# Two attention layers on one core: convolutions in idle score banks, a projection spread over the second layer, and the eighth chunk's values made in the next image

## What is computed

```python
# layer 0: 32-channel q and k, 256-channel v, softmax over axis 1
q = einsum('oc,bcn->bon', Wq, xf) + bq;  k = ... Wk;  v = ... Wv
attn = softmax(einsum('bci,bcj->bij', q, k), axis=1)
x = gamma * einsum('bcn,bnm->bcm', v, attn) + xf
# layer 1: phi and g are pooled 2x2, so that there are 1024 keys
theta = conv1x1(x);  phi = maxpool2(conv1x1(x));  g = maxpool2(conv1x1(x))
attention = softmax(theta^T phi, axis=-1)
y = gamma * conv1x1(g . attention) + x
```

## Time and profile before

| | |
|---|---|
| median of 3 runs (lowest, highest) | 2952.17 us (2945.66, 2953.29) |
| profiled execution, whole | 2952.56 us |
| its span, first to last instruction | 2950.8 us |
| mean granted TensorE clock | 0.967 of full |
| PE busy | 2757.0 us (93%) |
| DVE, POOL, ACT busy | 2008.1, 1949.9, 1750.7 us |
| longest waits of PE, in total | for prob_l 37.0 us, for vl 25.7 us, for psums 20.0 us |

### The profile page before, as it was taken

One profiled execution on the slowest core, in us unless ns is written; L12 is line 12 of the kernel. 1 busy time (PEld: TensorE's weight loads), 2 busy tenths in 40 slices (PEclk: granted clock), 3 DMA queues, 4 the chain that ended last, 5 costly groups with the idle time before them and its releaser, 6 DMA issues.

```text
span 2950.8 us, 39091 instructions
## 1 busy us (share of the span) xinstructions
PE 2757.0 (93%) x12260; PEld 2180.1 (74%) x12260; DVE 2008.1 (68%) x3303; ACT 1750.7 (59%) x3171; POOL 1949.9 (66%) x1480
## 2 busy tenths in 40 slices
PE   5899999989999999998999999999799999999978
PEld 4677777766677777776667777777666777777756
DVE  4577767756767677675776776777576767777665
ACT  3455565555665655555676565565566556555657
POOL 2366666765676667764677677666567766666658
PEclk7799999998999999999899999999999999999989
DMA  2000000011210000001120000000111000000011
GB/s 88 22 15 15 15 15 15 22 36 36 72 50 15 15 15 22 22 15 36 51 68 34 15 22 22 15 15 15 44 58 58 23 21 15 15 15 15 15 35 65
DMA packets 44280, 87.10 MB, mean 30 GB/s; under 512 B 2736, under 2 KB 2864, under 8 KB 44080
## 3 DMA queue, kind: packets, MB, share of 16 engines
q1 hardware_dynamic: 35360, 68.17, 6.8%
q10 hardware_dynamic: 8720, 16.46, 1.9%
HBM read 51.06 MB, written 33.55 MB: 29 GB/s over the span
## 4 chain that ended last, share of the span: by engine, by line
PE 77%; issue 9%; DVE 5%; ACT 5%; POOL 4%; DMA 1%; POOLq 0%; ACTq 0%; DVEq 0%
PE o_ps L797 30%; PE o_ps L775 16%; PE s_ps L765 8%; PE aux L828 8%; POOL prob_l L427 3%; PE aux L808 3%; PE aux L841 2%; ACT prob_h L490 2%; DVE mx L650 2%; PE aux L837 2%; PE aux L845 1%; PE aux L812 1%; PE aux L862 1%; PE o_ps L828 1%; PE o_ps L862 1%
## 5 line engine op out<-in xcount | busy, mean ns | idle before, releaser
L427 POOL TENSOR_TENSOR prob_l<-prob,prob_h 128x512 fp32r<-128x512 f32 x1280 | 1639.7, 1289 | 751.6 <-ACT prob_h L490 744.2
L487 ACT ACTIVATE prob<-s_ps 128x512 f32<-128x512 f32 x1280 | 768.5, 600 | 974.2 <-PE s_ps L765 973.5
L650 DVE TENSOR_REDUCE mx<-aux 128x1 f32<-128x512 f32 x1115 | 769.5, 690 | 459.3 <-PE aux L828 458.0
L797 PE MATMUL o_ps<-prob_h,vh 128*128 128x512 f32 x2304 | 935.8, 406 | 17.5 <-issue 12.6
L797 PE MATMUL o_ps<-prob_h,vl 128*128 128x512 f32 x2304 | 904.6, 393 | 0.0
L612 DVE TENSOR_TENSOR acc<-prob,acc 128x512 f32<-128x512 f32 x1216 | 836.1, 688 | 45.4 <-ACT prob L487 34.2
L775 PE MATMUL o_ps<-prob_l,vh 128*128 128x512 f32 x2304 | 756.0, 400 | 37.4 <-POOL prob_l L427 37.0
L490 ACT ACTIVATE prob_h<-s_ps 128x512 fp32r<-128x512 f32 x1280 | 762.1, 595 | 0.0
L775 PEld LDWEIGHTS o_ps<-prob_l,vh 128*128 128x128 f32 x2304 | 437.4, 191 | 144.7 <-POOL prob_l L427 57.0
L797 PEld LDWEIGHTS o_ps<-prob_h,vh 128*128 128x128 f32 x2304 | 437.0, 190 | 124.3 <-issue 24.8
L765 PE MATMUL s_ps<-queries,keys 128*128 128x512 f32 x1280 | 509.2, 399 | 0.8 <-DVE queries L669 0.8
(11 more groups left out here) (91 smaller groups left out, 1997.9 us busy)
## 6 DMA issues: line engine op xcount, KB each, us to landing
xa<-x SPq DMA_DIRECT2D x32, 512.0 KB, 3.7
...
```

Source lines behind the costliest of these rows:

```text
L427: nc.gpsimd.tensor_tensor(out=prob_l[:, i, :], in0=prob[:, i, :], in1=prob_h[:, i, :].bitcast(f32), op=ALU.subtract).then_inc(pl_ready, 1)
L487: nc.scalar.activation(prob[:, i, :], s_ps[s][:, :], ACT.Exp).then_inc(p_ready, 1)
L650: ins = nc.vector.tensor_reduce(out=dst, in_=bank[:, :], axis=AX.X, op=ALU.max)
L797: last = mm(o_ps[ct][:, :], value(parts, l, t, ct), prob_h[:, h % RING, :], start=t == 0 and parts is vh, stop=False)
```

## The change

The work is the same: every engine has as many instructions of each kind, except that four loads of image 0 (its chunks 0 to 3, which were loaded into `xa` as well as into `xp`) fall away.

1. **Banks.** Jobs in the lists ahead of a tile may use all eight banks: S0, S1, S2 (`s_ps`), O0 (`o_ps0`) and A (`acc`) beside X0, X1 and Y. The first scores, the first product and the first `acc` copy after such a list wait until the last job on their bank is free (`LAST_ON`).
2. **Beginning.** The keys and values of image 0 go round X1, Y, S0, S1, S2 and the maxima round X0, O0, A. `X` stands two chunks ahead, and reads the first four chunks from `xa`; `xp` takes chunks 4 and 5, and only 6 and 7 are loaded later.
3. **Transition.** The list is written anew, with three chunks projected in it. `K1` goes ahead of `G1`, its keys' low part becomes a job of its own (`K1M`), and its queries (`K1Q`, `K1L`) come after the maxima. The maxima of chunk 1 and its `M` move into chunk 0's tiles.
4. **Layer 1.** Chunk 3 is projected in chunk 0's tiles. The jobs of chunks 4 to 7 stand one in four tiles, at place 3, and the values of chunk 7 (two `V0`) in tiles 9 and 14 of the next image's layer 0.
5. **Layer 0.** In each chunk `X` stands in tile 6 (was 7), `K1` in 10 (13), `G1` in 14 (10), `T1` in 16 (17); in chunk 7 `XB` in tile 22.

```diff
-X0, X1, Y = range(3)
+X0, X1, Y, S0, S1, S2, O0, A = range(8)
...
+    turn = [X1, Y, S0, S1, S2]
+    st_turn = [X0, O0, A]
+    begin = [Job("X", 0, 0, 0, 0), Job("X", 0, 0, 1, 0)]
     for c in range(NCH):
...
+        k, kl, v0, vl0, v1, vl1 = project0(0, c, [turn[(3 * c + i) % len(turn)] for i in range(3)])
+        st = [maxima(0, 0, 0, c - 1, s, st_turn[(4 * c + s) % 3]) for s in range(SUBS)] if c else []
+        begin += st[:2] + [k, v0, kl] + st[2:] + [vl0, v1, vl1]
+        if c + 2 < NCH:
+            begin.append(Job("X", 0, 0, c + 2, 0))
...
-                    put(g + 7, 1, Job("X", 1, b, c, 0))
-                    put(g + 10, 1, on(Job("G1", 1, b, c, 0), X1))
-                    put(g + 13, 1, on(Job("K1", 1, b, c, 0), X1))
...
+                    put(g + 6, 1, Job("X", 1, b, c, 0))
+                    put(g + 10, 1, on(Job("K1", 1, b, c, 0), X1))
+                    put(g + 11, 1, Job("K1K", 1, b, c, 0), Job("K1Q", 1, b, c, 0))
+                    put(g + 12, 1, Job("K1M", 1, b, c, 0), Job("K1L", 1, b, c, 0))
+                    put(g + 14, 1, on(Job("G1", 1, b, c, 0), X1))
...
-            k3, v30, v31 = project0(b + 1, 3, (Y, X1, Y))
...
+            k0, k0l, v00, v00l, v01, v01l = project0(b + 1, 0, (X1, Y, S0))
+            k1_, k1_l, v10, v10l, v11, v11l = project0(b + 1, 1, (S1, S2, X1))
+            k2, k2l, v20, v20l, v21, v21l = project0(b + 1, 2, (O0, Y, S1))
+            before[tile_no(1, b, 0)] = [
+                d1, k0, d2, v00, add, v01, rnd, k0l, v00l, v01l, k1_, v10, k1_l, v10l, v11, v11l,
+                k1, Job("X", 0, b + 1, 2, 0), k1k, g1, k1m, t1, *st, k2, m0, k1q, k1l, t1l, v20, k2l, v20l, v21, v21l,
+                Job("X", 0, b + 1, 3, 0)]
...
+            places = [(8 * n + t) for n in range(1, 7) for t in (1, 5)]
+            for c in range(4, NCH):
+                k, kl, v0, vl0, v1, vl1 = project0(b + 1, c, (X1, X1, X1))
+                at = places[3 * (c - 4):3 * (c - 3)]
+                put(g + at[0], 3, k)
+                put(g + at[0] + 2, 1, kl)
+                if c == NCH - 1:
+                    at = (0, PHASE[1] + 9, PHASE[1] + 14)
+                put(g + at[1], 3, v0)
...
-                    if k == 1 and p < B * NCH:
+                    if k == 1 and ASLOTS + PSLOTS <= p < B * NCH:
                         load_p(p)
...
+                if (begin_step(h, AHEAD), S0 + h % SRING) in LAST_ON:
+                    wait_free(pe, LAST_ON[begin_step(h, AHEAD), S0 + h % SRING])
                 mm(s_ps[h % SRING][:, :], keys[l][:, t * P:(t + 1) * P], queries[:, q_slot(l, b, n), :],
```

More of the change, by code:

```diff
@@ new lines, in make_plan @@
+        k1, g1 = on(Job("K1", 1, b, c, 0), X0), on(Job("G1", 1, b, c, 0), S0)
+        t1 = on(Job("T1", 1, b, c, 0), S0)
+        st = [maxima(1, b, 0, 1, s, (X1, Y, S1, S2)[s]) for s in range(SUBS)]
+        m0 = on(Job("M", 1, b, 0, 0), X1)
+        add, rnd = Job("N", *last, 0), Job("X", 1, b, c, 0)
+        k1k, k1q, k1m, k1l = (Job(name, 1, b, c, 0) for name in ("K1K", "K1Q", "K1M", "K1L"))
+        t1l = Job("T1L", 1, b, c, 0)
+        if more:
+            k0, k0l, v00, v00l, v01, v01l = project0(b + 1, 0, (X1, Y, S0))
[5 more added lines that the diff above has]
+                Job("X", 0, b + 1, 3, 0)]
@@ L230, in make_plan @@
                     put(g + 4 + s, 3, maxima(1, b, n + 2, 1, s, Y))
+            if more:
+                if n < NCH - 1:
+                    for s, (t, place, at) in enumerate(((0, 1, X1), (2, 3, Y), (3, 3, Y), (4, 1, X1))):
+                        put(g + t, place, maxima(0, b + 1, 0, n, s, at))
+                else:
+                    for s in range(SUBS):
+                        put(g + s // 2, 1, maxima(0, b + 1, 0, n, s, (X1, Y)[s % 2]))
+                    put(g + 4, 1, on(Job("M", 0, b + 1, 0, 0), Y))
+        if more:
+            g = tile_no(1, b, 0)
+            k, kl, v0, vl0, v1, vl1 = project0(b + 1, 3, (X1, X1, X1))
+            put(g + 1, 1, k)
+            put(g + 2, 1, kl)
+            put(g + 4, 3, v0)
+            put(g + 5, 1, vl0)
+            put(g + 6, 1, v1)
+            put(g + 7, 1, vl1)
+            places = [(8 * n + t) for n in range(1, 7) for t in (1, 5)]
[7 more added lines that the diff above has]
+                put(g + at[1], 3, v0)
+                put(g + at[1] + 2, 1, vl0)
+                put(g + at[2], 3, v1)
+                put(g + at[2] + 2, 1, vl1)
+            for c, t in ((4, 5), (5, 8 + 6), (6, 24 + 3), (7, 32 + 4)):
+                put(g + t, 1, Job("X", 0, b + 1, c, 0))
     tail = (1, B - 1, NCH - 1)
@@ L271 @@
         LAST_ON_Y[_job.b + 1 if _job.l else _job.b] = _job
+for _g, _jobs in BEFORE.items():
+    for _job in _jobs:
+        if _job in BANK and BANK[_job] >= S0:
+            LAST_ON[_g, BANK[_job]] = _job
 def build(nc, x_d, w_d, wo_d, cols_d, y_d):
@@ L535, in entry @@
                                              bias=gbv[:, ct:ct + 1]).then_inc(xb_ready, 1)
-                elif name in ("K0", "K1"):
+                elif name in ("K0", "K1Q"):
                     q = queries[:, q_slot(l, b, c), :]
+                    if l:
+                        job = Job("K1", 1, b, c, 0)
+                        bank = aux[BANK[job]]
                     wait_full(act, job)
```

176 lines of the change are left out of this document (73 added, 103 removed).

## The result

The changed kernel takes 2871.48 us in the median of 4 runs (2867.30 to 2874.07), the kernel before 2948.91 us (4 runs, 2941.16 to 2953.29): a ratio of 0.9739 [0.9713, 0.9765]. The profiled execution took 2867.3 us; its span is 2865.5 us and its mean granted clock 0.983. Against the profiled execution before, 2952.56 us, that is a gain of 85.3 us; forecast were 109.5.

What follows compares the result with a forecast made beforehand. PE was taken to bound layer 0's full chunks, with gains only elsewhere. The terms -40 - 47 - 22.5 + 8.6 - 8.6 = -109.5 took 2952.56 us to 2843, range 2818 to 2876.

Steps and rivals of the forecast that it cites:

- the rival that layer 1 does not speed up: Layer 1, images 0 to 2: DVE takes PE's place as limit, no speedup; 2866 to 2873 us, chance 0.17.
- The beginning: Up to the first prob_h: 114.92 us becomes 75, four chunks of 5.8 us, two of 8.3; gain 40.
- The half clock feared here: Rival: the beginning stays at half clock, 93 us instead of 75; total 2861 us, chance 0.10.
- The transitions: Layer 0's last product to layer 1's first prob_h, images 0 to 2: 16, 16 and 15 us shorter.
- Pause (1): Transition: PE waits 1.5 us for DVE's pooling and K1M before the first ST.
- Pause (2): Transition: four reductions, the small ones and M, partly covered by chunk 2's K0, leave PE a 1.4 us pause.
- The third: Transition: layer 1's first scores wait for DVE's last V0L, a new PE wait of 2.9 us.
- Layer 1: Images 0 to 2: layer 1 gets 7.5 us shorter each, 22.5 in all; called the least certain term.
- of the 19 I leave 9: Layer 1's 19 us surplus falls to 9: about 5 for pauses and 4 for half clock.
- the 131.3 us of the base: Layer 1 after the change without surplus, scaled from seven chunks taking 91.55 us without a next image.
- The last transition: Image 3's transition to layer 1: 8.6 us shorter, from -9.5 in it and +0.9 for four ST in tiles.
- The clock rival: Clock holds where a fall was assumed: layer 1's surplus 4 instead of 9; 2822 us, chance 0.10.

Runs made afterwards that it cites:

- Experiment 7: The changed kernel with the last values of chunk 2 in the transition on bank A instead of a scores bank; 2871.11 us, ratio 0.9754 to the kernel before.
- experiments 5, 6, 9: The changed kernel with most of the next image's projections left out in layer 1: DVE's part, ACT's part, both; ratios to the kernel before 0.9719, 0.9709, 0.9650.
- experiment 2: The changed kernel with layer 1's projection jobs of chunks 4 to 7 bunched as before; 2876.91 us, ratio 0.9766 to the kernel before.
- experiment 3: The changed kernel with chunk 7's values made in layer 1 instead of the next image's first chunk; 2877.06 us, ratio 0.9769 to the kernel before.
- Experiment 10: The kernel before with ACT's copy of the column sums ahead of the exponentials of the tile two further on; 2892.77 us, ratio 0.9805.

## Why the prediction was right, and where it was wrong

The time, 2871, lies in the range, and the likeliest case was still not what happened: it was the rival that layer 1 does not speed up, priced at 2866 to 2873. Its price came true for half of its reason only. It named DVE alone; leaving out DVE's low parts takes 3.2 us of pauses an image away, leaving out ACT's writes 2.4. And "does not speed up" is a sum of two things that it did not tell apart: in three images half clock gave 11 us back (80.3 to 58.1 us, half of which counts), and the rest of layer 1 got 18 us longer. That these come to about nothing is luck.

- **The beginning: -40 forecast, -42.05 measured** (114.92 to 72.87). The period is 6.3 us and not 5.8, and in place of two of 8.3 there is one of 8.1:

```profile
35.32 0.74 DVE L651 SCALAR_TENSOR_TENSOR keys<-s_ps,cols,keys 32x512 fp32r<-32x512 f32 x1 [0.97 <-ACT queries L527]
41.63 0.74 DVE L651 SCALAR_TENSOR_TENSOR keys<-s_ps,cols,keys 32x512 fp32r<-32x512 f32 x1 [0.97 <-ACT queries L527]
49.73 0.74 DVE L651 SCALAR_TENSOR_TENSOR keys<-aux,cols,keys 32x512 fp32r<-32x512 f32 x1 [2.76 <-ACT queries L527]
...
42.85 0.39 ACTq L494 DMA_DIRECT2D xp<-x  x1
46.68 1.06 ACT L543 ACTIVATE xh<-xp 128x1024 fp32r<-128x1024 f32 x1 [3.24 <-DMA xp<-x]
```

  In each of the short periods DVE waits 0.97 us for ACT's queries; over the loop's 5.4 us the handovers come to 0.9, where I had put 0.4. The first late load costs 3.24 us of ACT and a period of 8.1; the second costs ACT 2.07 us, which the slack of the next job takes up. The half clock feared here did not come: the mean is 0.96, against 0.75 in the earlier trace rows.
- **The transitions: -16, -16, -15 forecast; -14.7, -17.7, -15.8 measured** with chunk 7 in front. Pause (1) of the forecast, 1.5 us, is 1.33 in two pieces, 0.87 before the transpose and 0.46 before the first maximum. Pause (2), 1.4, is 0.31 before `M` in image 0, where PE fills it with K0 at half clock, and 1.17 in image 2:

```profile
614.71 0.30 PE L887 MATMUL s_ps<-ident,gpool 128*128 128x128 f32 x1 [0.87 <-DVE gpool L655]
615.47 0.47 PE L863 MATMUL aux<-keys,queries 96*128 96x512 f32 x1 [0.46 <-DVE keys L651]
619.21 1.08 PE L868 MATMUL aux<-ident_r,nm_wide 128*128 128x128 f32 x4 [0.31 <-DVE nm_wide L681]
```

  The third, 2.9, is 1.69 in image 0 and 2.38 in image 2. My mechanism for it named DVE's last low part, and that is what the row says; but I let it hold up the first `prob_h` "whichever of the three banks tile 0 has", and in image 2 the first `prob_h` comes before that wait is over. Experiment 7 took the wait away and won nothing. ACT's queue, with the split of chunk 3 ahead of the exponentials, was its second cause, close behind.
- **Layer 1: -22.5 forecast, +6.9 measured. This is the step that failed**, the term "of the 19 I leave 9". Above the 131.3 us of the base the surplus is 16.0, 16.6 and 22.6 us. Of it, 6.8, 8.5 and 13.7 are half clock (forecast: 4), and 9.1, 8.1 and 8.9 are pauses and the rest (forecast: 5). The split has a flaw of its own: the 91.55 us from which the base is scaled hold 7.7 us at half clock, so the base was never free of it. Of the 19 us before, half clock explains about 9 (13.3 us lost by the records, less 4.4 that the base already has) and not 15. Without the clock (the estimate above) layer 1 went from 134.0 to 140.0 us in the mean of three images, of which 2.3 is work that moved in. I had argued that pauses would be few since DVE would be at 110 of 140 us. Its 109.95 us were right; ACT has 101.42 and POOL 106.00 beside it, each in a fixed order, and the two queues that I cut shorter gave back 3.2 and 2.4 us of pauses an image, together 5.5 (experiments 5, 6, 9). Shares of 69 to 75% on three engines that wait for each other did not hide the new work, as I had argued they would. That spreading the jobs would thin out the crowd was wrong for pauses (experiment 2: none fewer); of the 10 us in three images by which it is ahead in the profiles, 5 are half clock's.
- **First chunks: +2.85 forecast, +2.59 measured.** Whether they pay for themselves experiment 3 leaves open, as its difference is the clock's.
- **The last transition: -8.6 forecast, as -9.5 in it and +0.9 behind it; -10.5 and +1.0 measured.** It also has 10.5 us less at half clock than before (19.6 to 9.1), which the forecast did not count on. The +1.0 is a balance: the four `ST` forecast there come in, PE's pauses are 0.6 us longer (`Z` waits twice for the maxima of chunk 7, 0.32 us each), and half clock costs 1.6 us less than before; the rows do not name the rest.
- **Full chunks: 0 forecast, 0 measured** (66.42 and 66.44).
- The clock rival, 2822, let layer 1's half clock vanish. It fell from 80.3 to 58.1 us in three images, and rose from 24.0 to 27.3 in image 2.

So the profile after differs from the forecast mainly in layer 1: 29.4 us are missing there, and elsewhere 5 us more came than forecast.

**The clock** is what stays open. In the changed kernel the same place of layer 1, a wait of PE for `prob_l` at the start of chunk 1, looks like this in image 0 (first two windows) and in image 2 (last two):

```profile
650.28:653.69 3.41, 2.06 (x13) 1.76 (x13) 2.88 (x8) 2.31 (x5) 3.41 (x4) 1.00 0.36 126
653.69:657.11 3.42, 3.42 (x18) 2.69 (x17) 2.69 (x4) 1.49 (x4) 3.08 (x3) 1.00 0.00 0
2064.20:2067.61 3.41, 2.26 (x13) 1.52 (x12) 3.20 (x8) 2.27 (x5) 3.41 (x4) 1.00 0.55 154
2067.61:2074.44 6.83, 6.83 (x21) 5.25 (x21) 3.23 (x6) 1.97 (x4) 3.70 (x3) 0.50 0.00 0
```

PE was busy less in image 0, 2.06 us, and kept its clock; it was busy 2.26 us in image 2 and fell to half for 6.83 us. No pause in either window is over 1.4 us. The plan is the same but for the banks, which rotate from image to image, so the plan alone does not tell where the clock falls, and I did not find what does. Experiment 10 shows that it is not the sum of the pauses either: they stayed, and the half-clock time more than halved. The Trainium skill, "TensorE: Matmul & The Clock Gate", section "HAM oscillation — how this bites in real kernels", ties such falls to waits of several microseconds; these runs do not agree: in the kernel before no pause of PE in the three layer 1 stretches is over 0.94 us, and 24.0 to 29.1 us of each are at half clock; in the changed kernel none is over 1.9 us, but for the 2.38 us with which layer 1 begins in images 1 and 2.
